# Image channel two of the first sixteen chunks issued from ScalarE's queue

## What is computed

```python
def tok(X, W, b, class_token, pos_embed):
    patches = X.reshape(B, C, 8, 28, 8, 28).transpose(0, 2, 4, 1, 3, 5).reshape(B, 64, 3 * 28 * 28)
    tokens = jnp.einsum('bpi,hi->bph', patches, W) + b
    return jnp.concatenate([cls, tokens], axis=1) * pos_embed

h = tok(x, ...)
h = h + attention(layernorm(h), ...)      # over the batch axis, per position
h = h + experts(layernorm(h), ...)        # softmax over tokens, top 1024 of each expert, gelu, weighted scatter
```

## Time and profile before

| | |
|---|---|
| median of three runs | 929.53 us |
| the profiled execution, its own time | 934.2 us |
| its span | 932.0 us |
| PE busy | 758.7 us (81%) |
| DVE busy | 547.6 us (59%) |
| ACT busy | 446.2 us (48%) |
| POOL busy | 465.3 us (50%) |
| moved by DMA | 124.70 MB |

### The profile page before, as it was taken

One profiled execution on the slowest core, in us unless ns is written; L12 is line 12 of the kernel. 1 busy time (PEld: TensorE's weight loads), 2 busy tenths in 40 slices (PEclk: granted clock), 3 DMA queues, 4 the chain that ended last, 5 costly groups with the idle time before them and its releaser, 6 DMA issues.

```text
span 932.0 us, 13716 instructions
## 1 busy us (share of the span) xinstructions
PE 758.7 (81%) x4819; PEld 590.9 (63%) x4819; DVE 547.6 (59%) x1239; ACT 446.2 (48%) x734; POOL 465.3 (50%) x478
## 2 busy tenths in 40 slices
PE   1698998999999999999999985561176998788780
PEld 1698887888888889788888873341134554444330
DVE  1212685887787798788788767745876432331110
ACT  2552766667666666766766652232540332212220
POOL 1313555555555564556545522411103778888885
PEclk9899999999999999999999988785557899888995
DMA  9978799899988999898899620000101234334432
GB/s 222 214 175 190 171 208 215 202 202 209 220 203 207 210 208 212 203 221 200 205 217 204 163 72 23 1 23 23 12 4 25 37 62 66 62 63 67 66 40 25
DMA packets 135055, 124.70 MB, mean 134 GB/s; under 512 B 17384, under 2 KB 125792, under 8 KB 134860
## 3 DMA queue, kind: packets, MB, share of 16 engines
q1 hardware_dynamic: 113600, 91.27, 42.9%
q0 software_dynamic: 18848, 31.58, 17.8%
q10 hardware_dynamic: 2540, 0.99, 0.5%
HBM read 87.99 MB, written 12.98 MB: 108 GB/s over the span
## 4 chain that ended last, share of the span: by engine, by line
PE 28%; DVE 26%; POOL 20%; issue 16%; ACT 5%; DMA 3%; ACTq 1%; another core or an unknown queue 0%; SPq 0%; DVEq 0%; POOLq 0%
PE bank L1401 11%; POOL out L641 9%; POOL XS L631 5%; DVE Y L995 4%; PE bank L1507 4%; DVE stats L945 3%; DVE QT L1069 2%; DVE O L937 2%; ACT XS L846 2%; POOL rsB L513 2%; PE bank L1492 2%; DVE ET L1001 2%; DMA XS<-in_L_attn_proj_h_w 2%; POOL rsA L513 2%; PE bank L1538 1%
## 5 line engine op out<-in xcount | busy, mean ns | idle before, releaser
L1401 PEld LDWEIGHTS bank<-XS,WT 126*128 126x128 f32 (+1 forms) x2432 | 305.3, 192 | 27.0 <-issue 26.2
L1401 PE MATMUL bank<-XS,WT 126*128 126x128 f32 (+1 forms) x2432 | 310.8, 285 | 11.5 <-DVE stats L933 6.3
L697 ACT ACTIVATE XS<-XS 84x1152 f32<-84x1152 f32 (+1 forms) x192 | 184.5, 1034 | 0.1
L588 POOL COPY XS<-XS 84x1152 f32<-84x1152 f32 x64 | 89.7, 1402 | 67.7 <-DMA XS<-in_x 35.4
L641 POOL DMA_INDIRECT out<-XS x64 | 102.9, 1608 | 27.1 <-issue 19.1
L631 POOL DMA_INDIRECT XS<-token_rows,XS x64 | 65.2, 1019 | 54.5 <-DVE XS L1274 35.6
L995 DVE TENSOR_TENSOR_SCAN Y<-qdec,XT 128x512 f32<-128x512 f32 (+1 forms) x68 | 77.8, 1165 | 2.5 <-ACT XT L733 2.5
L875 ACT ACTIVATE XS<-bank,VT 128x512 f32<-128x512 f32 x64 | 43.7, 687 | 68.3 <-PE bank L1619 67.7
L601 POOL DMA_DIRECT2D XS<-XS x118 | 66.5, 566 | 17.3 <-POOL XS L588 17.3
L1619 PE MATMUL bank<-XS 128*128 128x512 f32 x128 | 68.4, 683 | 1.1 <-ACT XS L733 0.8
L1001 DVE SCALAR_TENSOR_TENSOR ET<-Y,ema_c,ET 128x512 f32<-128x512 f32 (+1 forms) x68 | 62.7, 923 | 1.8
(11 more groups left out here) (244 smaller groups left out, 1318.1 us busy)
## 6 DMA issues: line engine op xcount, KB each, us to landing
XS<-in_x SPq DMA_DIRECT2D x192, 392.0 KB
XS<-XS POOLq DMA_DIRECT2D x118, 189.0 KB, 7.6
out<-O SPq DMA_DIRECT2D x16, 256.0 KB, 9.3
token_rows<-XR SPq DMA_DIRECT2D x16, 256.0 KB, 8.9
XS<-in_L_ffn_W SPq DMA_DIRECT2D x16, 256.0 KB
XS<-in_L_tok_W SPq DMA_DIRECT2D x1, 1176.0 KB, 9.7
XS<-token_rows,XS POOLq DMA_INDIRECT x65, 3.7
out<-XS POOLq DMA_INDIRECT x64
```

The source lines that it names most:

```text
L588: pool.tensor_copy(ST[0:ROWS, n % 2, :, :, :].rearrange("p m j r -> p m r j"), px[:, :, :, PASSES:PATCH])\
L697: ins = act.activation(area(slice(0, ROWS), k // 4, piece, m0, m0 + CCOL // 2).rearrange("p m j r -> p m r j"), px[:, :, :, REST * piece:m ...
L1401: ins = pe.matmul(TOK[half][:, c0:c0 + CCOL], weights, pixels, start=(t == 0), stop=(t == passes_of(n) - 1))
```

## The change

For the first sixteen chunks (`SHARED = 2 * CHUNKS`, with `CHUNKS` = 8) SyncE issues channels 0 and 1 only. ScalarE issues channel 2: that of chunk 0 ahead of its 23 small DMAs, those of chunks 1 and 2 behind them, and that of chunk n + 3 after its third copy piece of chunk n, for n = 0 to 12, with a wait for `copied` and `staged` of chunk n ahead of it. Chunks 16 to 63 are loaded as before.

```diff
             def load_chunk(n):
 
                 if n < CHUNKS * NP:
-                    for c in range(C):
+                    for c in range(C - 1 if n < SHARED else C):
                         sp.dma_start(raw(n, c), rows_of(n % CHUNKS, n // CHUNKS, c)).then_inc(load[n % RING].sem, 16)
@@
+            def load_last(n):
+
+                act.dma_start(raw(n, C - 1), rows_of(n % CHUNKS, n // CHUNKS, C - 1)).then_inc(load[n % RING].sem, 16)
+
+            load_last(0)
             for v, row, n in vectors:
@@
             act.dma_start(lnb[:, :], bass.AP(ln_b.tensor, 0, [[0, 128], [1, D]])).then_inc(c_loaded.sem, 16)
+            for n in range(1, RING):
+                load_last(n)
@@
                 if piece == C - 1:
                     ins.then_inc(copied.sem, 1)
+                    if n + RING < SHARED:
+                        act.wait_ge(*copied.done(n))
+                        act.wait_ge(*staged.done(n))
+                        load_last(n + RING)
```

More of the change, by code:

```diff
@@ L429, in run, with rows_of, raw @@
                 iteration(NP, ((None, group(NP - 1, 1)),), False)
+        def rows_of(k, hy, c):
+            return x[CHUNK * k:CHUNK * k + CHUNK, c, ds(hy * PATCH, PATCH), :].rearrange("b p w -> p b w")
+        def raw(n, c):
+            return RAW[c:ROWS:C, n % RING, :].rearrange("p (b w) -> p b w", b=CHUNK)
+        SHARED = 2 * CHUNKS
         @block.sync
         def _(sp):
[L434 to L438, removed]
             def load_chunk(n):
                 if n < CHUNKS * NP:
-                    for c in range(C):
+                    for c in range(C - 1 if n < SHARED else C):
                         sp.dma_start(raw(n, c), rows_of(n % CHUNKS, n // CHUNKS, c)).then_inc(load[n % RING].sem, 16)
```

## The result

The changed kernel takes 959.68 us (median; 958.56 to 961.45, four runs), the kernel before 928.83 us (median of four; one run was added to the three). The ratio is 1.033, with a 95% interval of 1.029 to 1.037: about 31 us slower, where 11 were forecast. The time lies outside the range. In what follows a ratio leaves out single executions over 1.5% above the fastest of their kernel, and each of these is named where it bears on the argument.

A forecast was written before the change was run, and what follows sets the result against it. TensorE was taken as the bound, with the DMA engines nearly full early on. Start +7, relu wait and its clock price +4.4, later issues 0: +11.4 on the 929.5 us median gives 941 us, range 933 to 951.

The forecast's parts named there:

- Prologue: Start to first pixel pass: ScalarE's added issues and chunk 1's later landing delay its copy of chunk 1; +7 us.
- the high bound: Start of the kernel: constants delayed 3.1 us instead of 1 by chunk 0's channel, making the first pass +10.0 us later.
- The wait before the relu: Class tokens' relu: ScalarE first waits for POOL's copy of chunk 5 and issues chunk 8's DMA; TensorE stalls 3.0 us.
- The price of the gap: Behind TensorE's stall at the class tokens' relu: a lower clock costs 1.5 us more, making +4.4 us with the stall.
- an upper bound, 4.5 us: Class tokens' relu: most that TensorE's stall and the clock drop behind it should cost; 3.0 us without a clock drop.
- my three signs of being wrong: First pixel pass before 37 us, no TensorE stall at the class tokens' projection, or a delay at 80 us gone by 200.
- The other waits: ScalarE's waits at chunks 3, 4, 7 and 8: covered, so 0; up to 5 us if that cover were gone.
- The issues among later stages: Issues of chunks 12 and 15, 98 to 152 us: 1.6 us absorbed by a later 2.66 us gap; 0, at most 1.6.
- The first: Rival: chunk 1's channel 2 is not late, so at the start only issues count; 2.2 + 4.4 = 6.6, 936 us; chance 0.16.
- its mark of 26: Deciding sign for chunk 1's channel 2 not being late: ScalarE's copy of chunk 1 starts before 26 us.
- The second: Rival: ScalarE's queue fills up, holding two early issues up to 4.52 us each; 16 + 4.4 = 20.4, 950 us; chance 0.12.
- the third: Rival: not slower; two queues feed the DMA engines better, closing the gap before chunk 16; -4.2, 925 us; chance 0.08.

The follow-up runs named there:

- The first three chunks alone: Kernel before, with ScalarE issuing channel 2 of chunks 0, 1 and 2 only and SyncE all the rest: 935.56 us against 934.21, ratio 1.002.
- the filled gap: Changed kernel, with three throw-away TensorE multiplications (128 rows, 512 columns) ahead of its wait for the class tokens' relu: 944.17 us against 934.21, ratio 1.010.
- the burst over full rows: Kernel before plus ScalarE's wait for POOL's copy of chunk 5 ahead of the relu, then 24 TensorE multiplications over 128 rows: 943.39 us against 932.89.
- the two bursts over 84 rows: Kernel before plus ScalarE's wait ahead of the relu, then 84-row multiplications: 24 of 128 columns (944.41 to 970.14 us) or 6 of 512 (969.38, 969.56 us).

## Why the prediction was wrong, step by step

*Prologue, forecast +7 us: right in kind, twice too large.* The first pass came 3.6 us later. All the steps are in the trace: two issues behind the constants take 4.14 us together, the copy of chunk 0 ends at 23.8, the copy of chunk 1 waits for its load. But it starts at 26.97 us, and I had 30.4. The term that was mis-sized is the rate at which ScalarE's queue delivers its last packets. I took 146 packets per us from 12 to 20 us. In the changed kernel this is the same (1174 in 8 us), but between 20 and 28 us SyncE's queue runs dry. From 24 us on it moves no packet, and ScalarE's has the engines to itself:

```profile
q10 hardware_dynamic: 2055, 1.23, 71.1%
q1 hardware_dynamic: 677, 0.58, 30.4%
```

2055 packets in 8 us are 257 per us; in the kernel before it was 982 in the same 8 us, beside 1776 of SyncE's. I had named this ("it may run dry near 25 us") and still stayed near the high bound. Another 1.0 us came back on VectorE, where the decay table (`qdec`) took 1.24 us and not 2.26. The first three chunks alone cost 2.1 us in the whole, and in that run too ScalarE's copy of chunk 1 waits for its load and starts at 27.27 us.

*The wait before the relu: right to a quarter of a microsecond.* Forecast 3.0 us of gap, measured 2.75.

*The price of the gap: the step that failed.* "So 1.5 us more. The work behind my stall is of the same kind." It was not. The passes behind the gaps of the earlier trace rows cover 126 rows (126x128); behind this one come chunks 4 to 7, over 84 rows. The price was 22 us and not 1.5. What I had called an upper bound, 4.5 us, was no bound: it came from the only two gaps in the trace, and both were followed by the other shape. What the trace of before could have told, and I did not ask, is that no 84-row pass in it ever started with a low clock. So it did not show what such passes do with one. The runs showed it: the filled gap (+9), the burst over full rows (+9.3), and the two bursts over 84 rows, in whose profiles the clock is still at 0.50. None of my three signs of being wrong came up (the first pass started at 37.80 us and not before 37, L1489 stalled, the delay stayed), and "the passes behind it should be slow" was so. The list had no sign for how long they would be slow.

The Trainium skill ("TensorE: Matmul & The Clock Gate", section "What's actually happening") says that the throttled state is the default and that activity releases it. This trace agrees for 126 rows and not for 84: TensorE was busy for all of 64 to 110 us, and the clock stayed at 0.50. The same page of the Trainium skill ("Seeing it yourself") warns that the clock events of a trace may be unreliable. Here they are borne out by durations, 8.31 against 4.71 us for the same 38 instructions. Ahead of the first recorded change they are not: the row of 18 to 24 us of the kernel before says 1.00, but at 20.72 us two transposes take 0.64 us where at 94.08 us four take 0.60.

*The other waits, forecast 0: right.* ScalarE computed nothing for 6.7 us behind its copy of chunk 7 (the wait for POOL's copy and the issue) and for longer behind that of chunk 8, and TensorE had no gap from it in 64 to 113 us.

*The issues among later stages, forecast 0 since a later gap absorbs them: right in this trace.* Each of the two opened a gap of 0.76 us on TensorE (131.00 and 146.56 us), and the delay grew from 28.2 us at chunk 8 to 29.9 at chunk 12. Then the 2.66 us ahead of chunk 16 and the low clock behind it (30 instructions in 5.33 us, now 3.77) were gone, and the delay went down to 26.8, more than these issues had cost.

*The rivals.* The first came nearest for the prologue (+2.2 forecast, +3.6 at the first pass, +2.1 in the whole), though ScalarE's copy of chunk 1 started at 26.97 us and so missed its mark of 26. The second's mechanism, ScalarE held on its issues, was there with 4.14 us for two and not 9.0. Its sum takes 16 us for the prologue, of which the text derives 9.8 (7.4 and 2.4); the rest is put down to a late copy of chunk 2 without a figure, and no run shows it. Of the third one step occurred, the closed gap ahead of chunk 16; that it closes just as well when TensorE comes 1.8 us earlier (0.42 us, no DMA moved) says that two queues are not needed for it. Its time did not occur. No rival had the long stretch at the low clock. The rule of the Trainium skill cited in the prediction ("DMA: Bandwidth & Descriptors", section "Issuing engines are not separate DMA queues") leaves a second issuer only the sequencer's time to save. This trace agrees: in 12 to 20 us the changed kernel moved 1.87 MB and the kernel before 1.83, in 20 to 28 us 1.81 and 1.84.

## What to carry to other kernels

A gap on TensorE costs its length and, if the clock falls, half of the speed until work comes that brings it back. Look at the shape of the work behind the gap before taking the price of a gap from elsewhere in the trace. An in-order engine that issues DMAs takes their waits as well: put such a wait behind whatever another engine needs soon (here one relu, 26 us), and where a short wait of TensorE can't be avoided, a throw-away multiplication over all 128 rows in it is cheap (0.9 us here). One over fewer rows was not tried as a filler.

## What was not expected of the hardware

- At the level of 1.2 GHz, TensorE was busy without a break for 49 us with instructions over 84 rows and 128 columns (but for four others between two chunks at most), in another kernel for 10.45 us with ones of 512 columns, and the clock stayed there. 48 instructions over 128 rows in the same place, in all 6.9 us, brought it to 2.4 GHz before their end. Two of six executions with 48 instructions over 84 rows had, by their times, the full clock afterwards; whether it had fallen in them is open. Work over 84 rows that began at 2.4 GHz stayed at it, from 50 to 85 us of the kernel before.
- Gaps at one and the same place: 1.02 us, no fall in eight runs; 1.88 us, by the times a fall in all four runs of one kernel and a low clock afterwards in four of six of another; 2.75 us, a fall in four of four. At another place the clock stayed at 1.00 behind 2.54 us.
- A queue gets more of the engines when the other is empty: ScalarE's moved 147 packets per us beside 134 of SyncE's (12 to 20 us of the changed kernel), and 257 beside 85 (20 to 28 us).
